# Item projection of a two-sided graph layer: interleaved with the first adjacency group, or ahead of it

## What is computed

```python
h = item_feat @ W_item.T + b_item        # 10000 x 128, the "item projection"
b = x @ W_user.T + b_user                # 10000 x 128
z = x + relu(adj @ h + b)                # adj is 10000 x 10000, float32
out = layernorm(z)                       # over the 128 features, eps 1e-5
```

## Time and profile before

| what | us |
|---|---|
| median of three runs | 1103.01 |
| lowest and highest of them | 1102.78, 1103.82 |
| the profiled execution | 1102.25 |
| its span, first to last instruction | 1100.5 |
| PE busy | 1089.7 (99%) |
| DVE busy | 944.2 (86%) |
| ACT busy | 807.5 (73%) |
| POOL busy | 57.8 (5%) |
| DMA, mean of the span | 379 GB/s |

### The profile page before, as it was taken

One profiled execution on the slowest core, in us unless ns is written; L12 is line 12 of the kernel. 1 busy time (PEld: TensorE's weight loads), 2 busy tenths in 40 slices (PEclk: granted clock), 3 DMA queues, 4 the chain that ended last, 5 costly groups with the idle time before them and its releaser, 6 DMA issues. The chain is left out here.

```text
span 1100.5 us, 14565 instructions
## 1 busy us (share of the span) xinstructions
PE 1089.7 (99%) x5009; PEld 908.1 (83%) x5009; DVE 944.2 (86%) x682; ACT 807.5 (73%) x584; POOL 57.8 (5%) x29
## 2 busy tenths in 40 slices
PE   8999999999999999999999999999999999999997
PEld 7878888888888888888888888888888888888887
DVE  6889988888888888888888888888888888888876
ACT  5677877777777777777777777676767777777765
POOL 5870000000000000000000000000000000000000
PEclk9999999999999999999999999999999999999999
DMA  9999999999999999999999999999999999999996
GB/s 344 371 361 408 390 423 388 387 391 398 373 404 372 403 376 376 404 395 371 389 385 403 374 381 395 393 379 395 383 387 385 386 388 393 381 393 379 396 265 198
DMA packets 76324, 417.15 MB, mean 379 GB/s; under 512 B 8784, under 2 KB 19328, under 8 KB 30224
## 3 DMA queue, kind: packets, MB, share of 16 engines
q1 hardware_dynamic: 76160, 416.75, 97.8%
q10 hardware_dynamic: 144, 0.13, 0.0%
HBM read 411.67 MB, written 5.18 MB: 379 GB/s over the span
## 5 line engine op out<-in xcount | busy, mean ns | idle before, releaser
L505 DVE TENSOR_TENSOR adj_lo<-adj,adj_hi 128x2048 fp32r<-128x2048 f32 (+2 forms) x399 | 868.9, 2192 | 112.5 <-ACT adj_hi L380 110.0
L380 ACT CAST adj_hi<-adj 128x2048 fp32r<-128x2048 f32 (+2 forms) x399 | 731.1, 1833 | 261.7 <-PE acc L321 212.7
L315 PE MATMUL acc<-adj_hi,h_hi 128*128 128x512 f32 (+1 forms) x1580 | 608.2, 386 | 1.6 <-ACT adj_hi L386 1.6
L316 PE MATMUL acc<-adj_hi,h_lo 128*128 128x512 f32 (+1 forms) x1580 | 604.9, 384 | 0.0
L321 PE MATMUL acc<-adj_lo,h_hi 128*128 128x512 f32 (+1 forms) x1580 | 419.6, 385 | 0.8 <-DVE adj_lo L512 0.6
L315 PEld LDWEIGHTS acc<-adj_hi,h_hi 128*128 128x128 f32 x1580 | 296.8, 188 | 59.6 <-POOL h_lo L467 1.7
L316 PEld LDWEIGHTS acc<-adj_hi,h_lo 128*128 128x128 f32 x1580 | 296.9, 188 | 57.5
L321 PEld LDWEIGHTS acc<-adj_lo,h_hi 128*128 128x128 f32 x1580 | 292.5, 188 | 61.6 <-DVE adj_lo L505 2.3
L467 POOL TENSOR_TENSOR h_lo<-h_full,h_hi 128x512 fp32r<-128x512 f32 (+1 forms) x20 | 53.7, 2690 | 21.6 <-ACT h_hi L394 21.3
L523 DVE BATCH_NORM_STATS2 stats<-z_ps 128x6 f32<-128x128 f32 x79 | 17.6, 286 | 29.2 <-PE z_ps L331 29.2
L415 ACT ACTIVATE items<-z_ps,shift,rstd 128x128 f32<-128x128 f32 x79 | 29.7, 457 | 0.4 <-DVE shift L541 0.4
(11 more groups left out here) (31 smaller groups left out, 63.4 us busy)
## 6 DMA issues: line engine op xcount, KB each, us to landing
adj<-adj_t SPq DMA_DIRECT2D x360, 1024.0 KB, 7.4
adj<-adj_t SPq DMA_DIRECT2D x21, 512.0 KB, 5.4
adj<-adj_narrow SPq DMA_DIRECT2D x19, 544.0 KB, 5.3
items<-item_t SPq DMA_DIRECT2D x19, 256.0 KB, 4.7
xg<-x_t SPq DMA_DIRECT2D x19, 256.0 KB, 4.5
out<-items SPq DMA_DIRECT2D x19, 256.0 KB, 7.4
tail_in<-adj_tail SPq DMA_DIRECT2D x57, 32.0 KB, 4.1
adj<-adj_narrow SPq DMA_DIRECT2D x1, 272.0 KB, 3.8
```

Source lines behind the costliest of these rows:

```text
L315: nc.tensor.matmul(into, h_hi[:, k, :], adj_hi[:, s, c, 0:u], start=(k == 0), stop=False)
L316: nc.tensor.matmul(into, h_lo[:, k, :], adj_hi[:, s, c, 0:u], start=False, stop=False)
L380: nc.scalar.copy(adj_hi[:, s, start:, 0:u], adj[:, a, start:, 0:u]).then_inc(hi_made, 1)
L505: nc.vector.tensor_tensor(adj_lo[:, s, start:, 0:u], adj[:, a, start:, 0:u], adj_hi[:, s, start:, 0:u].bitcast(F32), ALU.subtract).then_in ...
```

## The change

- All twenty item tiles are loaded ahead of the adj tiles in SP's queue, into fourteen slots: six of their own (`OWN_SLOTS`) and eight in the space of adj tiles 3 and 4 (`item_tile`), four item tiles in each. Item tiles 14 to 19 use a slot a second time and wait for the product of the tile that had it. The two halves of adj tile 0 go ahead of item tiles 16 and 18 (`LOAD_HALF_BEFORE`). The loads of adj tiles 3 and 4 wait for the products of the item tiles in their space.
- PE projects all twenty item tiles before its first adj matmul.
- `h_full` is now whole, 78 chunks, and lies in the same memory as `h_lo`: POOL subtracts in place. DVE no longer waits for POOL to free a slot of it. The tail chunk has tiles of its own, `h_tail` and `items_tail`.
- ACT and DVE do their shares of the projection first; the halves of adj tile 0 are put in after item tiles 11 and 13 on ACT and after 13 and 15 on DVE; ACT splits adj tile 1 after item tile 17. The cast of the user weights moves from just before tile 19 to before tile 2.
- PE's warm-up uses a matrix of ones that DVE sets first, in place of POOL's identity, and has seven matmuls in place of five. POOL clears `items_tail` right at the start.

```diff
-ITEM_RING = 4
-H_RING = 4
 H_PS_RING = 4
-LEAD = 4
-WARM = 5
+WARM = 7
+OWN_SLOTS = 6
+GUEST_FROM = 3
+GUESTS = (ADJ_RING - GUEST_FROM) * PER_TILE
+ITEM_SLOTS = OWN_SLOTS + GUESTS
+LOAD_HALF_BEFORE = (16, 18)
+HIGH_HALF_AFTER = (11, 13)
+LOW_HALF_AFTER = (13, 15)
+HIGH_1_AFTER = 17
...
+        def item_tile(t):
+
+            at = t % ITEM_SLOTS
+            if at < OWN_SLOTS:
+                return items[:, at, :]
+            guest = at - OWN_SLOTS
+            return adj[:, GUEST_FROM + guest // PER_TILE, guest % PER_TILE, :]
...
             def load_items(t):
-                if t >= ITEM_RING:
-                    sp.wait_ge(h_product, t - ITEM_RING + 1)
+                if t >= ITEM_SLOTS:
+                    sp.wait_ge(h_product, t - ITEM_SLOTS + 1)
...
             def load_adj(g, t):
                 if later(g, 1) or t >= ADJ_RING:
                     sp.wait_ge(lo_made, steps_to(g, t - ADJ_RING))
+                elif t >= GUEST_FROM:
+                    sp.wait_ge(h_product, OWN_SLOTS + (t - GUEST_FROM + 1) * PER_TILE)
...
-            for t in range(LEAD):
+            for t in range(TILES):
+                if t in LOAD_HALF_BEFORE:
+                    load_first_half(LOAD_HALF_BEFORE.index(t))
                 load_items(t)
-            load_first_halves()
...
+            load_items_tail()
+            for t in range(1, TILES):
...
             def warm_up():
 
+                pe.wait_ge(warm_ready, 1)
+                for b in range(WARM):
+                    nc.tensor.matmul(z_ps[:, b % BLOCKS, :], warm[:, :], warm[:, :], start=True, stop=True)
...
-            for t in range(LEAD):
+            for t in range(TILES):
                 project_items(t)
             for t in range(TILES):
-                if t >= 1 and t + LEAD - 1 < TILES:
-                    project_items(t + LEAD - 1)
...
-            for t in range(LEAD - 1):
+            for t in range(TILES):
                 split_h(t)
-            split_hi_half(0)
-            split_hi_half(1)
-            for t in range(1, TILES):
-                if t == LAST:
-                    act.wait_ge(weights_landed, 16)
-                    nc.scalar.copy(h_hi[:, USER, :], w_user).then_inc(w_hi_made, 1)
+                if t in HIGH_HALF_AFTER:
+                    split_hi_half(HIGH_HALF_AFTER.index(t))
+                if t == HIGH_1_AFTER:
+                    split_hi(0, 1)
+            act.wait_ge(weights_landed, 16)
+            nc.scalar.copy(h_hi[:, USER, :], w_user).then_inc(w_hi_made, 1)
+            for t in range(2, TILES):
                 split_hi(0, t)
-                if t + LEAD - 2 < TILES:
-                    split_h(t + LEAD - 2)
...
             def add_item_bias(t):
...
-                if t >= H_RING:
-                    dve.wait_ge(h_lo_made, t - H_RING + 1)
...
-            for t in range(LEAD):
+            for t in range(TILES):
                 add_item_bias(t)
-            split_lo_half(0)
-            split_lo_half(1)
+                if t in LOW_HALF_AFTER:
+                    split_lo_half(LOW_HALF_AFTER.index(t))
             for t in range(1, TILES):
                 split_lo(0, t)
-                if t + LEAD - 1 < TILES:
-                    add_item_bias(t + LEAD - 1)
```

More of the change, by code:

```diff
@@ L137, in gnn_kernel @@
         h_hi = sb("h_hi", [P, USER + 1, HID], F32R)
+        with nc.sbuf_tensor("h_full", [P, USER + 1, HID], F32) as h_full:
+            pass
         h_lo = sb("h_lo", [P, USER + 1, HID], F32R)
         h_pack = sb("h_pack", [P, HID], F32R)
-        h_full = sb("h_full", [P, H_RING, PER_TILE, HID])
-        items = sb("items", [P, ITEM_RING, PER_TILE * P])
+        h_tail = sb("h_tail", [P, HID])
+        items = sb("items", [P, OWN_SLOTS, PER_TILE * P])
+        warm = sb("warm", [P, P])
         w_all = sb("w_all", [P, 2 * HID + 2])
@@ L150, in gnn_kernel @@
         shift = sb("shift", [P, BLOCKS])
-        items_tail = items[:, LAST % ITEM_RING, LAST_FULL * P:LAST_FULL * P + P]
+        items_tail = sb("items_tail", [P, P])
         z_t = items[:, 0, :]
@@ L166, in gnn_kernel @@
         half_landed = sem("half_landed")
-        item_landed = [sem(f"item_landed{i}") for i in range(ITEM_RING)]
+        item_landed = [sem(f"item_landed{i}") for i in range(ITEM_SLOTS)]
         items_tail_landed = sem("items_tail_landed")
@@ L204, in load_items @@
             def load_items(t):
[L205 to L206 removed]
+                if t >= ITEM_SLOTS:
+                    sp.wait_ge(h_product, t - ITEM_SLOTS + 1)
                 n = full_chunks(t) * P
[L208 to L209 removed]
+                sp.dma_start(item_tile(t)[:, 0:n],
+                             item_t[:, t * PER_TILE * P:t * PER_TILE * P + n]).then_inc(item_landed[t % ITEM_SLOTS], 16)
             def load_items_tail():
@@ L229, in load_adj, with load_first_half @@
                              full_rows[:, t * PER_TILE:t * PER_TILE + n, :]).then_inc(adj_landed[t % ADJ_RING], 16)
-            def load_first_halves():
-                for (a, b), landed in zip(HALVES, (half_landed, adj_landed[0])):
-                    sp.dma_start(adj[:, 0, a:b, :], adj_t[0, :, a:b, :]).then_inc(landed, 16)
+            def load_first_half(half):
+                a, b = HALVES[half]
+                sp.dma_start(adj[:, 0, a:b, :], adj_t[0, :, a:b, :]).then_inc(adj_landed[0] if half else half_landed, 16)
             def load_x(g):
@@ L280, in warm_up, with spread_bias @@
             def warm_up():
+                pe.wait_ge(warm_ready, 1)
+                for b in range(WARM):
+                    nc.tensor.matmul(z_ps[:, b % BLOCKS, :], warm[:, :], warm[:, :], start=True, stop=True)
+            def spread_bias():
                 pe.wait_ge(ident_ready, 1)
-                for b in range(WARM):
-                    nc.tensor.matmul(z_ps[:, b % BLOCKS, :], ident[:, :], ident[:, :], start=True, stop=True)
-            def spread_bias():
                 pe.wait_ge(weights_landed, 16)
@@ L298, in project_items @@
                 for c in range(n):
-                    mm = nc.tensor.matmul(h_ps[t % H_PS_RING][:, c, :], items[:, t % ITEM_RING, c * P:c * P + P],
+                    mm = nc.tensor.matmul(h_ps[t % H_PS_RING][:, c, :], item_tile(t)[:, c * P:c * P + P],
                                           w_item, start=True, stop=True)
@@ L302, in project_items @@
                     pe.wait_ge(items_tail_landed, 16 * len(PACKS))
-                    mm = nc.tensor.matmul(h_ps[t % H_PS_RING][:, n, :], items_tail, w_item,
+                    mm = nc.tensor.matmul(h_ps[t % H_PS_RING][:, n, :], items_tail[:, :], w_item,
                                           start=True, stop=True)
@@ L470, in _ @@
             pool.wait_ge(h_lo_made, TILES)
-            nc.gpsimd.tensor_tensor(h_pack[again, :], h_full[again, LAST % H_RING, LAST_FULL, :],
+            nc.gpsimd.tensor_tensor(h_pack[again, :], h_tail[again, :],
                                     h_pack[again, :].bitcast(F32), ALU.subtract).then_inc(h_pack_made, 1)
@@ L556, in group @@
                         mean_shift(g - 1)
+            nc.vector.memset(warm[:, :], 1.0).then_inc(warm_ready, 1)
             nc.vector.memset(tail_in[:, :], 0.0).then_inc(tail_in_zeroed, 1)
```

31 lines of the change are left out of this document (12 added, 19 removed).

## The result

| | before | after |
|---|---|---|
| median of 20 runs (lowest to highest), us | 1103.13 (1102.18 to 1104.88) | 1101.74 (1100.71 to 1102.28) |
| profiled execution, its span, us | 1102.25, 1100.5 | 1101.29, 1099.5 |
| tail matmul of group 0 (M), us from the span's start | 80.92 | 80.35 |

The ratio of after to before is 0.9986, with a 95% interval of 0.9979 to 0.9992: 1.4 us earlier by the medians, less than the 2.2 us that I had called the bound of "no change"; the interval leaves out 1, so the gain is small but real. The forecast was 1103.0 in a range of 1097.8 to 1105.0.

The account below looks back on a forecast made before the run. PE was taken to bound the kernel, so only M could move. 74.9 without waits, plus waits 2.0, 1.6 and 2.4 and clock 0.7, gave 81.6, +0.7 on 1102.25: 1103.0 us, range 1097.8 to 1105.0.

Parts of the forecast that it names:

- Only M counts: From group 1 on PE alone sets the time, so the end moves only with M, 80.92 before.
- Projection in one piece, ending 22.7: PE projects all items without starving on loads, ending at 22.7; the borrowed adj space costs nothing.
- Rival D: In the projection, items load slower than they are projected, PE waits for each tile: +4, 1106; chance 0.05.
- The cast of adj tile 1: wait 2.0: ACT casts adj tile 1 only after the cast of h 17, at 25.4; PE waits 2.0 us.
- Its low part: wait 1.6: DVE's low part of adj tile 1 waits for POOL and ends at 30.6; PE waits 1.6 us.
- Four waits of 0.6: In adj tiles 2 to 5 a DVE and POOL pair takes 3.31 against PE's 2.72; waits total 2.4 us.
- The clock: 0.7 between 0 and 1.5: Slow passes at the projection's start, after the new warm-up, cost 0.7 us, the middle of 0 to 1.5.
- my 81.6: The predicted time of M in the changed kernel, 81.6 us, against 80.92 before.
- B: During POOL's backlog in the first adj tiles, DVE is not held up: M at 76.7, 1098; chance 0.15.
- C: From the first half of adj tile 0, POOL keeps DVE out while anything is queued: 1106.8; chance 0.11.
- the 0.76: The runs' median of before lay 0.76 us above its profiled execution; nothing was added, a later clock switch would explain it.
- My +0.7 on the span: The predicted net shift of M and so of the end, 0.7 us later than before.

Follow-up runs that it names:

- no_lock: The changed kernel with POOL's twenty `h_lo` subtractions replaced by clears, the low part of h left out of the result: 1097.23 us, ratio 0.9944.
- best: The changed kernel with POOL's `h_lo` operations spread out and the casts of adj tiles 1, 2 and 3 made early: 1097.41 us, ratio 0.994.
- run 4: The same run as no_lock: the changed kernel with POOL's twenty `h_lo` subtractions replaced by clears: 1097.23 us, ratio 0.9944.
- run 9: The kernel before, unedited, profiled three more times on another chip: 1104.97, 1103.51 and 1103.96 us.
- control: The changed kernel again, no edit, on the same chip as the other variants: 1101.60 us, ratio 0.9991 to the kernel before.
- early_hi: The changed kernel with ACT's cast of adj tile 1 after item tile 15 in place of 17: 1100.65 us, ratio 0.9977.
- extra_pool: The changed kernel with five more POOL subtractions after the twenty, into a spare tile: 1103.30 us, ratio 1.0.
- paced: The changed kernel with POOL's `h_lo` from item tile 13 on let in one after every second low part: 1099.05 us, ratio 0.9953.
- look 1: The kernel before, unedited, first of three further profiled executions: 1104.97 us, M at 83.93.
- look 3: The kernel before, unedited, third of three further profiled executions: 1103.96 us, M at 82.35.
- new_warm: The kernel before with only the new warm-up, seven matmuls on DVE's matrix of ones: 1103.60 us, ratio 1.0001.
- look 2: The kernel before, unedited, second of three further profiled executions: 1103.51 us, M at 82.40.
- run 2: The changed kernel with the old warm-up, five matmuls on POOL's identity: 1102.08 us, ratio 0.9989.

## Why the prediction was right, point by point

- **Only M counts.** Right. After M the two profiles differ by 0.4 in the span, 0.3 of it in the last group, by as much as two executions of one kernel do, and in the eight kernels of runs 1 to 8 the time follows M (76.75 to 82.93): their medians are M plus 1019.8 to 1021.2.
- **Projection in one piece, ending 22.7.** Measured 22.60. The borrowed adj space and the longer row of item loads cost nothing in after. The cover is thinner than I had said: in no_lock PE waited 0.7 and in best 1.0 for item loads during the projection. Rival D has its place there, at a quarter of its price; after itself shows nothing of it.
- **The cast of adj tile 1: wait 2.0.** Measured 1.57. The cast started at 24.95, I had 25.4, since POOL was ahead of my count and DVE's second half was done at 23.19 and not at 23.5.
- **Its low part: wait 1.6.** Measured 1.37, from the same early DVE start (26.88, I had 27.3).
- **Four waits of 0.6.** Four of 0.42 to 0.45 with 0.11 at each restart, 0.55 in all. DVE's low parts start 3.27 to 3.31 apart, for a predicted 3.31. This step decided the case, and runs 4 to 6 show it from three sides: without POOL's reads the waits go, with five more there are five more, and with the same number spread out they go. The Trainium skill, SBUF — State Buffer, Who interferes with whom, calls it an exclusive lock and has issue order decide; the 3.27 to 3.31 here and the 2.29 of run 4 agree with it.
- **The clock: 0.7 between 0 and 1.5.** It took 0: passes are fast from 4.9. That is more than half of the 1.25 by which M came before my 81.6; the cast's wait is 0.4 of it and the low part's 0.2, and the four waits another 0.2 (these add to 1.5, against which stand about 0.3 of rounding and restarts that I had not counted). That it took 0 in after is partly luck: the other profiles with the new warm-up have between 0 and 8 slow passes, 0 to 0.8, inside my bounds. The middle of them was a choice without a row. What made it come out low on average is the edit of the warm-up (about 0.6, run 9) and not the move of the projection.
- **B, that DVE isn't held up.** Refuted by the 3.34 at 26.88. **C, that POOL keeps DVE out.** Refuted by the 1.39 at 18.35. Both rivals lived on a row that before lacked, DVE asking while POOL has another operation ready.
- **What failed: the time of before as the base.** I added nothing for the 0.76 by which before's median lay above its profiled execution, and named a later clock switch as its likely reason. The traces speak against it: of the four profiles of before mine had the latest switch (8.0 against 5.4 to 7.4). What the others have in its place is a second fall of the clock, during or just after PE's two waits between 9.5 and 13.5, in two of three further looks, and in the third other waits; M in all three is 82.3 to 83.9. The fall isn't the whole reason for the median either. 3.4 us at half the clock are 0.0015 of a run, so none with a mean granted clock of 0.999 can have it, and the eight such runs of before beside control took 1103.5 to 1103.9, with a median of 1103.7, above the 1103.58 of all. The rest of the cause is open. I had written that the wait of 1.6 before the first adj matmul "did not do that", which is true of one execution. Counted from a typical before, at M of about 82.4, after gains 2 and not 0.57; the medians say 1.4, and 2.0 in run 1. My +0.7 on the span was of the wrong sign, and inside the bound only because all the terms are small. Leaving out the 0.76 was luck: with it the forecast would have been 1103.8, 2.1 from the 1101.74 measured and not 1.3. Taken from a typical M of 82.4, the same sum (81.6) would have said 0.8 earlier than before.

**Left open.** Whether the clock can fall in after's own waits of 1.57 and 1.37. No trace has it. But the mean granted clock of every run is on record: two of control's eleven runs took 1105.4 and 1105.5 with a clock of 0.995 and 0.996, where the other nine have 0.998 to 0.999; one of early_hi's ten took 1104.3 and one of extra_pool's ten 1105.9, both with 0.995, where the others have 0.997 to 0.999. A lack of 0.003 to 0.004 of 1100 us is 3.3 to 4.4, about what these four lie above their medians (2.6 to 3.9). So in these four a clock at half speed somewhere accounts for the lost time; at which point of the program isn't shown. (One of after's twenty has 0.948 at an ordinary 1101.69, so that this figure proves nothing without the time.) The nine runs of paced and best have none like it; nor have after's twenty by their times. Long waits can't be all of the condition, since early_hi's first two are 0.70 and 0.45 and paced has one of 1.68.

## What to carry to other kernels

Before putting a producer phase ahead of a consumer phase, ask which two engines were kept apart by the old mixing. Here the phase took no longer, but its by-product was a queue of POOL work that took turns with DVE's full low parts for 17 us (26.9 to 44.0); letting POOL in after every second low part gave 2.5 us more than the move by itself (1101.60 to 1099.05), and with earlier casts 4.2. And take several executions of the kernel before as the base when a forecast turns on one microsecond: one profile can be a lucky one. Four of this kernel had the same matmul at 80.92, 82.35, 82.40 and 83.93.

## What the runs showed of the hardware

- **PE's clock can fall in two waits of which neither is long.** In before's look 1 PE waited 1.22 and 0.82 by the brackets, in look 3 1.58 and 0.99, in new_warm 1.58 and 1.00, and the granted clock was 0.50 for about 3.4 us just after; in the profiled execution (1.58 and 0.59) and in look 2 (1.58 and 0.77) it stayed at 1.00. The price was up to eight matmuls at 0.43 in place of 0.227, some 1.6 us. The Trainium skill, TensorE: Matmul & The Clock Gate, What's actually happening, says that the point of a switch differs from run to run; the first rise, between 5.4 and 8.0 in these five executions, agrees.
- **DVE's low parts (two SBUF inputs) and POOL's subtractions take strict turns, one operation each**, even when POOL's next one stands ready. A full low part ends about 2.15 after POOL's operation and POOL's 1.14 to 1.16 after DVE's, in one tile after the other from 26.88 to 43. A POOL clear of the same size, which reads nothing, ran inside a low part and left DVE at its 2.29 (run 4).
- **The column PEclk shows 1.00 from the start**, in the slow passes too: 11 passes in 2 us and 21 in 2 us have the same entry in run 2. In these profiles the clock before the first fall must be read from the distance of starts.
- **The first rise of the clock moves by 2.6 us between executions of one kernel.** With the warm-up starting at 1.53 each time, the passes of before were fast from 8.0, 6.2, 7.4 and 5.4 on. What an early rise won was partly lost again: the fall came in the executions with the rise at 5.4, 6.2 and 6.7, and not in those with 7.4 and 8.0. Five executions are few, and none of the runs sets the moment of the rise.
